# First attention of a 16-sample transformer kernel: weighed rows in two buffers in turn, and the product with the inverted sums two units later

## Chip, cores and metric

The kernel runs on one core of a Trainium2 chip. The metric is device time in microseconds of one execution of the whole program; before the change it was 1013.97 us, the median of three runs from 1012.39 to 1016.23 us.

## What is computed

A network of two layers on 16 samples of 256 tokens with 128 features, all in float32. Each layer modulates a layer norm, runs an attention, modulates again and runs a mixture of experts. The change lies in the attention of the first layer:

```python
xn = _ln(x, g_attn, b_attn)
qkv = (xn @ qkv_w + qkv_b)            # 16 heads of 8
scores = einsum("bhqd,bhkd->bhqk", q, k) / sqrt(HD)
scores = where(causal, -inf, scores)
attn_w = softmax(scores, axis=-1)
attn = einsum("bhqk,bhkd->bhqd", attn_w, v)
attn = attn @ out_w + out_b
```

What follows it in the layer (a residual, eight steps of a tanh recurrence, a feed-forward block and the experts) needs the attention of all samples in the order of the kernel's stages.

## The kernel before

Every engine has its own hand-written program; they meet at semaphores alone. Features lie on the 128 partitions, tokens in the columns. The samples are called batches, b = 0 to 15.

The first attention is one loop of 144 steps (`A_STEPS`), t = 0 to 143, that all engines walk through with the same counter. Eight steps make one batch; the step within a batch is the unit u = t % 8. A step handles two of the sixteen heads.

- TensorE. In step t it makes the row scores of two heads of batch t // 8 (`row_scores`, L445 and L452) into three PSUM banks in turn, and, 11 steps behind (`A_LAG`), the transposed scores of the same heads: first minus the maxima (`minus_maxima`, L465, the first instruction of a step in the rows below), then `key_scores` (L474, L477). `row_scores` waits for `a_mx`, the maxima three scores back, before it writes its bank. Behind these stands one more piece by unit: in even steps the weighing of values (`weigh`, L494), in u = 1 the transposition of the maxima (L418), in u = 3 the projection of values (L405), in u = 5 the projection of queries and keys of the next batch (`project_qk`, L388 and L389), in the steps of `OUT_STEPS` the output projection (`out_project`, L433), which waits for the product, `a_on`.
- VectorE. In step t it takes the maxima of the two heads (`maxima`, L1206 and L1208, each with a short read of the accumulator), 0.6 us a head. Ahead of the maxima of u = 4 stands `values` (L1229). Behind the maxima of the steps in `NORM_STEPS` stands `normalise` (L1244), called the product here: `ao = av * rec`.
- ScalarE. In step t it takes the exponentials of two transposed scores (`exps`, L918). Behind them stand, by step: `copy_maxima` (u = 1), `log_sums` (L932) and `exp_sums` (L936), which invert the sums as exp(-ln(x)), `keep_weighed` (L925, u = 4), which copies the weighed rows of batch b - 2 out of PSUM, `take_qk` (u = 5, L898 and L899), and `add_bias` (L940). TensorE's `minus_maxima` waits for an exponential of the step before.
- GpSimd. In step t it cuts the upper triangle from two heads' exponentials (`cut`, L1607, two instructions), and then masks queries of the next batch (`mask_queries`, L1616; u = 6 and 7, then 1 and 3) or adds a residual (L1621). The first step of a batch waits for the mask of u = 6 (`a_q`).
- SyncE's queue. The weighed rows hold values in 16 of every 32 partitions and their sums in the other 16. For batches 0 to 13 four DMAs (L297) move the sums beside the values, from `av` to `rec`, after `keep_weighed` (`a_cp`) and, as `rec` is one buffer, after the product of the batch before (`a_on`). For batches 14 and 15 VectorE does it with a shuffle (`spread_sums`, L1238). `log_sums` waits for the DMAs.

So the sums of a batch go: `keep_weighed` in u = 4, DMAs, logarithm in u = 0, exponential in u = 2, product in u = 3, output projection in u = 7 (batches 0 to 12, with the weighing two batches behind the row scores). `av`, `rec` and `ao` are one buffer each, 512 columns, in arrays that the layer norms use at other times.

Row scores end at step 127 (`A_UNITS`); steps 128 to 143 finish the transposed side. Batch 13 has its logarithm in step 128, exponential in 130, product and output projection in 131.

Of the kernel before, what the change touches and what calls it, by code (L numbers as in the profile page):

```python
# [14 lines left out]
ALU = mybir.AluOpType  # L15
ACT = mybir.ActivationFunctionType
# [3 lines left out]
BATCH, SEQ, D = 16, 256, 128  # L20
# [22 lines left out]
def adaln_kernel(nc, a):  # L43
    ctx = ExitStack()
    with ctx:
        def sb(name, shape, dt=FP32):
            return ctx.enter_context(nc.sbuf_tensor(name, shape, dt))

        def sem(name):
            return ctx.enter_context(nc.semaphore(name))  # L50
# [64 lines left out]
        sqb = sb("sqb", [P, 4, CH])  # L115
        rsb = sb("rsb", [P, 4, CH])
        xnb = sb("xnb", [P, 4, CH])
# [6 lines left out]
        mrow = sb("mrow", [P, 2, 3 * P], BF16)  # L124
        pr = sb("pr", [P, 6 * P])
        qs = sb("qs", [P, 2, SEQ])
        av, rec, ao = sqb[:, 0, :], rsb[:, 0, :], xnb[:, 0, :]

        lf, lw = qm[:, :, 0:2, :], qm[:, :, 2:4, :]
        av1, rec1, ao1 = sqb[:, 0:2, :], rsb[:, 0:2, :], xnb[:, 0, :]  # L130
# [28 lines left out]
        PS = ctx.enter_context(nc.psum_tensor("PS", [P, 8, CH], FP32))  # L159
# [14 lines left out]
        a_t, a_p, a_cut, a_av, a_cp, a_sh = [sem("a_" + n) for n in ("t", "p", "cut", "av", "cp", "sh")]  # L174
        a_moved = [sem(f"a_moved{n}") for n in range(2)]
        a_inv, a_on, a_pj, a_att, a_h = [sem("a_" + n) for n in ("inv", "on", "pj", "att", "h")]
# [30 lines left out]
        A_PST, A_PSO, A_PSM = 3, 6, 7  # L207
# [6 lines left out]

            return 4 + (q % 4 if q < 4 * STEPS else q % 2)

        NORM_STEPS = {8 * (b + 3) + 3 if b < BATCH - 2 else 8 * (b + 2) + 6: b for b in range(BATCH)}
        OUT_STEPS = {8 * (b + 3) + 7 if b < BATCH - 3 else 8 * (b + 3) + 3 if b < BATCH - 2 else 8 * (b + 2) + 7: b
                     for b in range(BATCH)}
        SPREAD_BY_DMA = BATCH - 2  # L220
        SPREAD_STEPS = {8 * (b + 2) + 5: b for b in range(SPREAD_BY_DMA, BATCH)}
        LOG_STEPS = {8 * (b + 3) if b < BATCH - 2 else 8 * (b + 2) + 5: b for b in range(BATCH)}
        EXP_STEPS = {8 * (b + 3) + 2 if b < BATCH - 2 else 8 * (b + 2) + 5: b for b in range(BATCH)}
        RESIDUAL_STEPS = {8 * (b + 4) + 2 if b < BATCH - 3 else 8 * (b + 3) + (5 if b < BATCH - 2 else 1): b
                          for b in range(BATCH - 1)}
        B_PSO, B_PSX = 6, 7
# [24 lines left out]
        def _(sp):  # L251
# [19 lines left out]
            for head in range(HEADS0):  # L271
                p = 32 * (head // 4) + HD0 * (head % 2)
# [11 lines left out]
            for head in range(HEADS1):  # L284
                p = 32 * (head % 4)
# [6 lines left out]
            for b in range(SPREAD_BY_DMA):  # L292
                sp.wait_ge(a_cp, b + 1)
                if b:
                    sp.wait_ge(a_on, b)
                for j in range(4):
                    sp.dma_start(rec[32 * j:32 * j + 16, :], av[32 * j + 16:32 * j + 32, :]).then_inc(a_moved[b % 2], 16)  # L297
            sp.wait_ge(a_av, 4 * BATCH)
            for dst, src in ((up0, a["up0"]), (gate0, a["gate0"])):
                sp.dma_start(dst, src).then_inc(ld_m0, 16)  # L300
# [556 lines left out]
        def _(act):  # L857
# [62 lines left out]

            def keep_weighed(b):
                act.wait_ge(a_av, 4 * b + 4)
                if b:
                    act.wait_ge(a_on, b)
                nc.scalar.activation(av[:, :], PS[:, A_PSO, :], ACT.Copy).then_inc(a_cp, 1)  # L925

            def log_sums(b):
                if b < SPREAD_BY_DMA:
                    act.wait_ge(a_moved[b % 2], 64 * (b // 2 + 1))
                else:  # L930
                    act.wait_ge(a_sh, b - SPREAD_BY_DMA + 1)
                nc.scalar.activation(rec[:, :], rec[:, :], ACT.Ln).then_inc(a_inv, 1)  # L932

            def exp_sums(b):
                act.wait_ge(a_inv, 2 * b + 1)
                nc.scalar.activation(rec[:, :], rec[:, :], ACT.Exp, scale=-1.0).then_inc(a_inv, 1)  # L936
# [6 lines left out]
            for t in range(A_STEPS):  # L943
                b, u, v = t // 8, t % 8, t - A_LAG
                if 0 <= v < A_UNITS:
                    exps(v)
                if u == 1 and 1 <= b <= BATCH:
                    copy_maxima(b - 1)
                if t in LOG_STEPS:
                    log_sums(LOG_STEPS[t])  # L950
                if t in EXP_STEPS:
                    exp_sums(EXP_STEPS[t])
                if u == 4 and b >= 2:
                    keep_weighed(b - 2)
                if u == 5 and b + 1 < BATCH:
                    take_qk(b + 1)
                if t in OUT_STEPS:
                    add_bias(OUT_STEPS[t])
# [155 lines left out]
        def _(dve):  # L1114
# [104 lines left out]
            def last_part(b):  # L1219
                dve.wait_ge(a_st, b + 1)  # L1220
                nc.vector.tensor_tensor(mxs[:, b % 2, :, :, :, 2], mxs[:, b % 2, :, :, :, 1], upper(b, 1),
                                        ALU.subtract).then_inc(a_sp, 1)
# [10 lines left out]
            def spread_sums(b):  # L1233

                dve.wait_ge(a_cp, b + 1)
                if b:
                    dve.wait_ge(a_on, b)
                nc.vector.stream_shuffle(rec[:, :], av[:, :], [16 + p % 16 for p in range(32)]).then_inc(a_sh, 1)  # L1238

            def normalise(b):  # L1240
                dve.wait_ge(a_inv, 2 * b + 2)
                if b:
                    dve.wait_ge(a_pj, b)
                nc.vector.tensor_tensor(ao[:, :], av[:, :], rec[:, :], ALU.mult).then_inc(a_on, 1)  # L1244

            dve.wait_ge(va_ones, 6)
            dve.wait_ge(mod_step, 10)
            for t in range(A_STEPS):
                b, u = t // 8, t % 8
                if t in SPREAD_STEPS:  # L1250
                    spread_sums(SPREAD_STEPS[t])
                if u == 4 and b < BATCH:
                    values(b)
                if t < A_UNITS:
                    maxima(t)
                if t == A_UNITS:
                    last_part(BATCH - 1)
                if t in NORM_STEPS:
                    normalise(NORM_STEPS[t])
                if u == 7 and b < BATCH:  # L1260
                    split_maxima(b)
# [509 lines left out]
```

## Time and profile before

| | |
|---|---|
| median of 3 runs | 1013.97 us |
| the profiled execution's own time | 1014.14 us |
| its span | 1012.3 us |
| instructions | 21410 |
| TensorE matmul busy | 930.3 us, 92% |
| VectorE busy | 616.3 us, 61% |
| ScalarE busy | 552.0 us, 55% |
| GpSimd busy | 460.2 us, 45% |
| granted TensorE clock, mean of the span | 0.989 |

Times in the rows are microseconds from the span's start, and every number is of one profiled execution. A busy TensorE is not TensorE at its peak: its matmuls are pipelined, and a short wait in the midst of a step may show as longer instructions instead of as idle time. The distance between the first L465 of two steps, a step's length, is the surer measure.

### The profile page before, as it was taken

Reading aid. Unit: us, or ns where it says so; the run is one execution under the profiler, and the core shown is the slowest. Engines: PE = TensorE matmul, PEld = TensorE weight load, DVE = VectorE, ACT = ScalarE, POOL = GpSimd, SP = SyncE. Lnnn points to the kernel's source line nnn. Section 1 sums busy time; section 2 is a strip of 40 time slices with the busy share of each in tenths; the row PEclk is TensorE's granted clock in tenths of the full one; section 3 lists DMA queues with packets and bytes.
Section 4 is the critical chain, followed back from the end, with each engine's and each line's share of the span. In section 5 each row is a group of like instructions: output and inputs, shape, how many; then the busy total and the mean of one; then the engine's idle time right before and its main releaser. Section 6 shows DMA issues by size and latency. Waiting matters only on the chain.

```text
span 1012.3 us, 21410 instructions
## 1 busy us (share of the span) xinstructions
PE 930.3 (92%) x7335; PEld 590.9 (58%) x7335; DVE 616.3 (61%) x2028; ACT 552.0 (55%) x1077; POOL 460.2 (45%) x697
## 2 busy tenths in 40 slices
PE   8999999999989979999887998889997899999997
PEld 4566677777654223334533886456664444399994
DVE  4788888888815966863633544577873653344444
ACT  6536666667657554565511554557785622255551
POOL 1146776776642946630074454335543044323331
PEclk9999999999999999999998999999999999999999
DMA  6720000000010000040011224100000000121115
GB/s 207 245 79 13 13 8 13 13 8 13 13 60 35 0 1 1 0 167 0 1 51 49 79 78 154 50 2 1 2 2 1 1 29 30 37 57 49 49 31 177
DMA packets 38617, 45.95 MB, mean 45 GB/s; under 512 B 7872, under 2 KB 31936, under 8 KB 37648
## 3 DMA queue, kind: packets, MB, share of 16 engines
q1 hardware_dynamic: 34000, 35.26, 11.4%
q0 software_dynamic: 4512, 9.32, 2.8%
q8 instruction: 62, 1.02, 0.4%
q14 instruction: 43, 0.35, 0.1%
HBM read 31.32 MB, written 18.69 MB: 49 GB/s over the span
## 4 chain that ended last, share of the span: by engine, by line
PE 78%; DVE 7%; ACT 6%; issue 4%; another core or an unknown queue 1%; DMA 1%; POOL 1%; DVEq 0%; SPq 0%; POOLq 0%
PE PS L697 6%; PE PS L452 5%; PE PS L494 5%; PE PS L680 5%; PE PS L687 5%; PE PS L348 4%; PE PS L465 4%; PE PS L640 3%; PE PS L357 3%; PE PS L631 3%; PE PS L633 3%; PE PS L554 2%; PE PS L445 2%; PE PS L790 2%; PE PS L809 2%
## 5 line engine op out<-in xcount | busy, mean ns | idle before, releaser
L918 ACT ACTIVATE pw<-PS 128x384 f32<-128x384 f32 x256 | 111.6, 488 | 73.0 <-PE PS L474 71.4
L1607 POOL TENSOR_SCALAR_AFFINE_SELECT pw<-pw 128x256 f32<-128x256 f32 x256 | 103.7, 429 | 75.8 <-ACT pw L918 74.6
L1206 DVE CUSTOM_DVE_ANT_0 PS<-PS,above 128x256 f32<-128x256 f32 x256 | 114.1, 446 | 38.4 <-PE PS L445 36.2
L1673 POOL DMA_INDIRECT token_rows<-xnb,slot_in x77 | 73.9, 959 | 114.2 <-ACT xnb L1032 107.6
L1659 POOL TENSOR_TENSOR XS<-XS,N 128x512 f32<-128x512 f32 x64 | 81.1, 1288 | 55.7 <-DVE N L1280 35.0
L452 PE MATMUL PS<-kf,qm 32*128 32x256 f32 x512 | 103.2, 426 | 0.5 <-POOL qm L1616 0.5
L1459 DVE TENSOR_TENSOR rsb<-sqb,PS 128x256 f32<-128x256 f32 (+1 forms) x77 | 42.6, 553 | 93.6 <-PE PS L687 44.8
L1208 DVE CUSTOM_DVE_ANT_0 PS<-PS,above 128x128 f32<-128x128 f32 x256 | 84.7, 331 | 0.0
L1629 POOL TENSOR_SCALAR_AFFINE_SELECT pw<-pw 128x256 f32<-128x256 f32 x128 | 56.0, 472 | 59.6 <-ACT pw L1077 59.6
L1015 ACT ACTIVATE sqb<-PS 128x512 f32<-128x512 f32 x48 | 28.7, 597 | 99.4 <-PE PS L631 80.6
L1370 DVE TENSOR_TENSOR rsb<-sqb,PS 128x512 f32<-128x512 f32 x48 | 32.9, 688 | 78.5 <-PE PS L633 55.9
L1616 POOL TENSOR_SCALAR qm<-qs,qmask 128x256 f32<-128x256 f32 x64 | 59.5, 931 | 43.8 <-ACT kf L899 43.8
L477 PE MATMUL PS<-qm,kf 32*128 32x256 f32 x512 | 76.3, 374 | 0.0
L1176 DVE TENSOR_TENSOR xnb<-PS,rsb 128x512 f32<-128x512 f32 x56 | 38.7, 691 | 56.5 <-ACT rsb L884 47.5
L1667 POOL DMA_INDIRECT sorted_rows<-H,pos x32 | 30.8, 964 | 79.7 <-DVE pos L1439 65.3
L1667 POOL DMA_INDIRECT sorted_rows<-region,pos x32 | 30.7, 959 | 77.1 <-DVE pos L1439 45.7
L680 PE MATMUL PS<-xnb,pw 128*128 128x128 f32 x460 | 64.1, 275 | 0.0
L687 PE MATMUL PS<-xnb,pw 128*128 128x128 f32 x460 | 63.9, 275 | 0.0
L970 ACT ACTIVATE PS<-PS,cols 128x512 f32<-128x512 f32 x64 | 42.2, 662 | 37.5 <-PE PS L554 22.3
L445 PE MATMUL PS<-kf,qm 32*128 32x128 f32 x512 | 61.7, 271 | 0.0
L445 PEld LDWEIGHTS PS<-kf,qm 32*128 32x128 f32 x512 | 60.7, 185 | 0.8
L554 PE MATMUL PS<-N,wxs 128*128 128x512 f32 x112 | 59.2, 615 | 2.0 <-DVE N L1289 0.4
(212 smaller groups left out, 2336.2 us busy)
## 6 DMA issues: line engine op xcount, KB each, us to landing
sorted_rows<-empty_rows_dram SPq DMA_DIRECT2D x2, 2535.0 KB, 14.7
slot_in<-sorted_rows SPq DMA_DIRECT2D x77, 65.0 KB
N<-token_rows SPq DMA_DIRECT2D x16, 256.0 KB, 5.0
X<-xT_dram SPq DMA_DIRECT2D x8, 256.0 KB, 5.2
token_rows<-empty_rows_dram SPq DMA_DIRECT2D x1, 2048.0 KB, 24.4
ATT<-gate_dram SPq DMA_DIRECT2D x1, 2048.0 KB
XS<-down_dram SPq DMA_DIRECT2D x1, 2048.0 KB
H<-up_dram SPq DMA_DIRECT2D x1, 2048.0 KB
```

The costliest lines, as they stand in the source:

```text
L445: nc.tensor.matmul(PS[:, bank, SEQ:SEQ + P], qm[r, b % 3, g, 0:P], kf[r, b % 3, 0:P], start=True, stop=True).then_inc(a_s, 1)
L452: nc.tensor.matmul(PS[:, bank, 0:SEQ], qm[r, b % 3, g, P:SEQ], kf[r, b % 3, :], start=True, stop=True)
L477: m = nc.tensor.matmul(PS[:, bank, 0:SEQ], kf[r, b % 3, 0:P], qm[r, b % 3, g, :], start=False, stop=True, skip_group_check=True)
L554: nc.tensor.matmul(PS[:, k, :], wxs[:, :], V[:, s], start=False, stop=True, skip_group_check=True).then_inc(i_p, 1)
L680: m = nc.tensor.matmul(PS[:, b, n * P:(n + 1) * P], wgate[:, b, n * P:(n + 1) * P], xnb[:, b, 0:P], start=True, stop=True)
L687: m = nc.tensor.matmul(PS[:, 2 + b, n * P:(n + 1) * P], wup[:, b, n * P:(n + 1) * P], xnb[:, b, 0:P], start=True, stop=True)
L918: nc.scalar.activation(pw[:, w % 2, j + n, :], PS[:, A_PST + (2 * v + n) % 3, 0:3 * P], ACT.Exp).then_inc(a_p, 1)
L1206: nc.vector.tensor_tensor_reduce(x[:, 0:SEQ], x[:, 0:SEQ], above[:, :], 1.0, -3e38, ALU.add, ALU.max, mxs[:, t // 8 % 2, 1, j, g, 0:1])
L1208: nc.vector.tensor_tensor_reduce(x[:, SEQ:SEQ + P], x[:, SEQ:SEQ + P], above[:, P:SEQ], 1.0, -3e38, ALU.add, ALU.max, mxs[:, t // 8 % 2, 0 ...
L1607: m = nc.gpsimd.affine_select(x[:, :, SEQ * k:SEQ * k + P], x[:, :, SEQ * k:SEQ * k + P], [[0, 2], [1, P]], ALU.is_ge, 0.0, base=0, channe ...
L1659: nc.gpsimd.tensor_tensor(XS[:, s], XS[:, s], V[:, s], ALU.add).then_inc(i_x, 1)
L1673: nc.gpsimd.indirect_dma_start(token_rows[l][:, :], bass.IndirectOffsetOnAxis(slot_in[:, r, D:D + 1].bitcast(mybir.dt.int32), 0), slot_out ...
```

## The change

`av` becomes two buffers in turn by batch. `keep_weighed` waits for the product of two batches before. The product goes from u = 3 to u = 5 for batches 0 to 12, and from step 131 to 130 for batch 13; the exponential of batch 13 goes from step 130 to 128. Batches 14 and 15 keep their steps (but batch 14 now lies in the other buffer).

```diff
-        av, rec, ao = sqb[:, 0, :], rsb[:, 0, :], xnb[:, 0, :]
+        av = [sqb[:, (b + 1) % 2, :] for b in range(BATCH)]
+        rec, ao = rsb[:, 0, :], xnb[:, 0, :]
...
-        NORM_STEPS = {8 * (b + 3) + 3 if b < BATCH - 2 else 8 * (b + 2) + 6: b for b in range(BATCH)}
+        NORM_STEPS = {8 * (b + 3) + (5 if b < BATCH - 3 else 2) if b < BATCH - 2 else 8 * (b + 2) + 6: b for b in range(BATCH)}
...
-        EXP_STEPS = {8 * (b + 3) + 2 if b < BATCH - 2 else 8 * (b + 2) + 5: b for b in range(BATCH)}
+        EXP_STEPS = {8 * (b + 3) + (2 if b < BATCH - 3 else 0) if b < BATCH - 2 else 8 * (b + 2) + 5: b for b in range(BATCH)}
...
-                    sp.dma_start(rec[32 * j:32 * j + 16, :], av[32 * j + 16:32 * j + 32, :]).then_inc(a_moved[b % 2], 16)
+                    sp.dma_start(rec[32 * j:32 * j + 16, :], av[b][32 * j + 16:32 * j + 32, :]).then_inc(a_moved[b % 2], 16)
...
             def keep_weighed(b):
                 act.wait_ge(a_av, 4 * b + 4)
-                if b:
-                    act.wait_ge(a_on, b)
-                nc.scalar.activation(av[:, :], PS[:, A_PSO, :], ACT.Copy).then_inc(a_cp, 1)
+                if b >= 2:
+                    act.wait_ge(a_on, b - 1)
+                nc.scalar.activation(av[b], PS[:, A_PSO, :], ACT.Copy).then_inc(a_cp, 1)
...
-                nc.vector.stream_shuffle(rec[:, :], av[:, :], [16 + p % 16 for p in range(32)]).then_inc(a_sh, 1)
+                nc.vector.stream_shuffle(rec[:, :], av[b], [16 + p % 16 for p in range(32)]).then_inc(a_sh, 1)
...
-                nc.vector.tensor_tensor(ao[:, :], av[:, :], rec[:, :], ALU.mult).then_inc(a_on, 1)
+                nc.vector.tensor_tensor(ao[:, :], av[b], rec[:, :], ALU.mult).then_inc(a_on, 1)
```

## Rows read from the trace of the kernel before

**Rows 1.** The page, part 4: the chain that ended last, shares by engine.
```profile
PE 78%; DVE 7%; ACT 6%; issue 4%; another core or an unknown queue 1%; DMA 1%; POOL 1%; DVEq 0%; SPq 0%; POOLq 0%
```
**Rows 2.** Timeline of TensorE, step 29: start, length, engine, line, operation, out<-in.
```profile
92.70 0.34 PE L465 MATMUL PS<-mrow,selb 32*128 32x384 bf16 x2
...
95.18 0.34 PE L465 MATMUL PS<-mrow,selb 32*128 32x384 bf16 x2
```
**Rows 3.** The same view, steps 21 and 22, before the first product.
```profile
78.38 0.34 PE L465 MATMUL PS<-mrow,selb 32*128 32x384 bf16 x2
...
80.36 0.33 PE L465 MATMUL PS<-mrow,selb 32*128 32x384 bf16 x2
```
**Rows 4.** Timeline of VectorE, end of step 27 and start of step 28.
```profile
91.48 0.76 DVE L1244 TENSOR_TENSOR xnb<-sqb,rsb 128x512 f32<-128x512 f32 x1
92.16 0.41 DVE L1229 TENSOR_TENSOR region<-PS,vb 128x256 f32<-128x256 f32 x1
92.50 0.42 DVE L1206 CUSTOM_DVE_ANT_0 PS<-PS,above 128x256 f32<-128x256 f32 x1
```
**Rows 5.** The same view, step 21 and the first maximum of step 22.
```profile
79.33 0.43 DVE L1206 CUSTOM_DVE_ANT_0 PS<-PS,above 128x256 f32<-128x256 f32 x1 [0.34 <-PE PS L445]
...
80.56 0.14 DVE L1208 DVE_READ_ACCUMULATOR2_ANT mxs<- 128x1 f32 x1
81.31 0.43 DVE L1206 CUSTOM_DVE_ANT_0 PS<-PS,above 128x256 f32<-128x256 f32 x1 [0.61 <-PE PS L445]
```
**Rows 6.** Timeline of GpSimd: cuts in step 21 and beside a product, a mask.
```profile
80.37 0.77 POOL L1607 TENSOR_SCALAR_AFFINE_SELECT pw<-pw 128x256 f32<-128x256 f32 x2 [0.93 <-ACT pw L918]
82.35 0.76 POOL L1607 TENSOR_SCALAR_AFFINE_SELECT pw<-pw 128x256 f32<-128x256 f32 x2 [1.22 <-ACT pw L918]
...
91.29 1.22 POOL L1607 TENSOR_SCALAR_AFFINE_SELECT pw<-pw 128x256 f32<-128x256 f32 x2 [0.94 <-ACT pw L918]
...
97.92 0.92 POOL L1616 TENSOR_SCALAR qm<-qs,qmask 128x256 f32<-128x256 f32 x1
```
**Rows 7.** Timeline of TensorE, first row of step 32.
```profile
98.90 0.33 PE L465 MATMUL PS<-mrow,selb 32*128 32x384 bf16 x2
```
**Rows 8.** Timeline of ScalarE: rows kept, logarithm, the exponentials behind it.
```profile
92.83 0.60 ACT L925 ACTIVATE sqb<-PS 128x512 f32<-128x512 f32 x1
...
100.72 0.63 ACT L932 ACTIVATE rsb<-rsb 128x512 f32<-128x512 f32 x1
101.78 0.87 ACT L918 ACTIVATE pw<-PS 128x384 f32<-128x384 f32 x2 [0.43 <-PE PS L474]
```
**Rows 9.** L297 on SyncE's queue: timeline, then issue and landing times of all 56.
```profile
93.45 3.06 SPq L297 DMA_DIRECT2D rsb<-sqb  x4
...
L297 SPq DMA_DIRECT2D rsb<-sqb x56: 507/589/983, 79.1 to 273.3; - x56
DMA to landing us min/median/max: 1.9/2.0/3.4
```
**Rows 10.** Timeline of TensorE: steps 33, 125 and 131.
```profile
100.61 0.34 PE L465 MATMUL PS<-mrow,selb 32*128 32x384 bf16 x2
...
102.41 0.34 PE L465 MATMUL PS<-mrow,selb 32*128 32x384 bf16 x2 [0.46 <-ACT pw L918]
...
270.69 0.34 PE L465 MATMUL PS<-mrow,selb 32*128 32x384 bf16 x2
...
272.92 0.34 PE L465 MATMUL PS<-mrow,selb 32*128 32x384 bf16 x2 [0.73 <-ACT pw L918]
...
283.24 1.13 PE L433 MATMUL PS<-xnb,wout 128*128 128x256 f32 x4 [0.65 <-DVE xnb L1244]
```
**Rows 11.** Timeline of ScalarE: exponentials of step 129, then the pair of step 133.
```profile
279.35 0.87 ACT L918 ACTIVATE pw<-PS 128x384 f32<-128x384 f32 x2 [0.32 <-PE PS L474]
...
287.80 0.63 ACT L932 ACTIVATE rsb<-rsb 128x512 f32<-128x512 f32 x1
...
289.00 0.85 ACT L918 ACTIVATE pw<-PS 128x384 f32<-128x384 f32 x2
```

## The prediction

> **What bounds the kernel now.** I read the page first: the chain that ended last is 78% matmul [rows 1], so a gain must shorten TensorE's own sequence. The change touches only the first attention, steps 0 to 143 (step 16 begins near 70 us, the stage ends near 304 us). There I read TensorE's timeline by the start of each step, which is the first L465 row of a step (t = 8b + u; u is the unit). A plain step is 1.7 us. In step 29 (u = 5) the start is at 92.70 and the next at 95.18, 2.48 us [rows 2]. Step 21 is the same unit with the same projection behind it, but comes before the first product, and takes 80.36 - 78.38 = 1.98 us [rows 3]. The 0.50 us between them is what the change can win in a batch.
>
> VectorE's timeline says where it comes from. The product of step 27 starts at 91.48, the value add of step 28 runs behind it, and the first maximum of step 28 starts at 92.50 [rows 4], so both take 1.02 us of VectorE. In a step with nothing else VectorE only has some 0.48 us to spare (0.34 us idle and a 0.14 us read that the next instruction may overlap) [rows 5]. The maxima of step 28 are therefore about 0.55 us late. They free the PSUM bank that the second row-score product of step 29 writes (TensorE waits for a_mx there), and everything after it in step 29 shifts: its transposed scores, then the projection, ScalarE's exponentials, the queries. TensorE is shown busy meanwhile; it is the step's length that gives the wait away.
>
> **The change, part by part.**
>
> Product of batches 0 to 11, from step u = 3 to u = 5 (steps 29, 37, ... 117): nothing is added, 0.77 us of VectorE moves. Taken away at u = 3 it leaves the value add (0.33 us) in a gap of 0.48 us: the maxima of u = 4 are on time and step u = 5 falls to 1.98 us. Put behind the maxima of u = 5 it finds the widest gap of the batch, because two projection passes sit between the scores of u = 5 and of u = 6: in step 21 the last read starts at 80.56 and the next maximum at 81.31 [rows 5], 0.75 us for an instruction whose successor starts 0.69 us later (91.48 to 92.16 by the value add, 0.77 us long itself). So it ends between 0.06 us before and 0.02 us after the next maximum is ready. Gain 0.50 us each, 12 x 0.50 = **6.0 us**. Bounds: 0.25 us if the new place costs half of what the old one did, 0.55 us if all the lateness comes back.
>
> GpSimd beside it. While the product of step 27 ran (91.48 to 92.25) the pair of cuts that began at 91.29 took 1.22 us; the pair at 80.37 in step 21 took 0.77 us [rows 6]. The product now starts at 80.56 of that clock against a pair at 80.37, the same 0.19 us behind, so the 0.45 us loss of GpSimd moves with it and does not grow. The next cuts wait for exponentials of u = 6 and start near 82.35, GpSimd being idle 1.22 us before them: that much cover for 0.45 us. Without that cover it would reach the mask of the next batch's queries, which does matter: the mask begun at 97.92 ends at 98.84, and step 32, whose scores need it, starts at 98.90 [rows 6, 7]. I cost it at nothing. The Trainium skill, SBUF - State Buffer, section "Who interferes with whom", says that a VectorE instruction with two SBUF inputs and a GpSimd instruction that reads SBUF exclude each other, and that the second to start blocks fully. By that the product would first wait 0.2 us for the running cut and end 0.1 to 0.2 us late for the maxima of u = 6; the row shows it only 0.08 us longer than the undisturbed one.
>
> Two buffers for the kept rows: the copy of batch b (L925, at 92.83 [rows 8]) waited for the product of b-1, which now comes two steps later; with the other buffer it waits for b-2, done a batch before. Cost nothing, same instruction. The cover is the buffer: with one, that copy, the first reader of the bank that the next weighing overwrites, would be stuck behind the product.
>
> The four DMAs that spread the sums (SP queue, one at a time) write the one buffer of inverted sums, so they still wait for the product of b-1. They started when the copy ended (93.45, step start + 0.75); they now start at the product's end, step start + 2.18 + 0.77 = + 2.95. From the first issue to the last landing: normally three issues of 0.59 and 2.0 us to land, 3.8 us; in this batch the issues took 3.06 us, so about 4.5 us [rows 9]. They land at + 6.8 to + 7.5. ScalarE wants them for the logarithm at 100.72, + 8.02 [rows 8], now + 7.52. It holds by 0.7 us, in the worst case seen by nothing, and behind the logarithm ScalarE sits idle 0.43 us. Cost 0; SP has nothing else queued there that is due before the stage ends.
>
> Product of batch 12, step 125: there is no projection in this step. Now it takes 272.92 - 270.69 = 2.23 us with TensorE waiting 0.73 us for ScalarE; a step of this kind with its wait for the exponentials and no late maxima is step 33, 1.80 us [rows 10]. Gain 0.43 to 0.55 us; I take **0.45**. Here the gap is a plain one of 0.48 us, so the product makes the maxima of step 126 late by 0.3 us. Their reader, the second score of step 127, has about that much to spare, since half of 0.55 us of lateness was absorbed at u = 5 too.
>
> Batch 13: exponential from step 130 to 128, product from 131 to 130, output projection unchanged at 131. TensorE waited 0.65 us there for the product [rows 10]; this goes. But logarithm and exponential now run back to back before the exponentials of step 129: such a pair takes 289.00 - 287.80 = 1.20 us, the logarithm alone 0.63 us, and the idle behind the lone logarithm in front of step 129 was 0.32 us [rows 11]. 1.20 - 0.63 - 0.32 = 0.25 us; TensorE waits for ScalarE in these steps, so this is given back. Net **0.40**. If the DMAs land late this is the place without slack.
>
> Sum: 6.0 + 0.45 + 0.40 = 6.85 us. What follows the stage (layer norms, recurrence, experts) hangs on its end in one chain and moves with it. The profiled execution took 1014.14 us for a span of 1012.3; that gives 1007.3. It lies 0.17 us over the median of the three runs, 1013.97. Forecast **1007.2 us**, 0.7% faster.
>
> **Rivals.**
>
> (a) The stall moves to u = 6 and 7: the product finishes late for the maxima of u = 6. For: the gap is 0.75 us for 0.69 to 0.77 us, and it shares with GpSimd. Against: 0.55 us of lateness costs 0.50 us today, so 0.1 us should hide wholly. If half comes back: 12 x 0.25 + 0.85 = 3.9 us, 1010.1. Chance 0.10.
>
> (b) GpSimd is held before the mask and step u = 0 starts 0.45 us later per batch: 12 x 0.05 + 0.85 = 1.5 us, 1012.5. It needs the product to run over the cuts of u = 6, over a microsecond later than I place it. Chance 0.04.
>
> (c) Slower: a ring product, DMA, logarithm, exponential, product through the single buffer of inverted sums. It decides when first issue to last landing takes more than 4.54 + 0.43 = 4.97 us, and makes the kernel slower beyond 5.5 us. If every batch had landings like the longest, 3.4 us, and issues as at 93.45 (2.5 + 3.4 = 5.9 us), it would lose 5.9 - 4.97 = 0.93 us a batch against a gain of 0.50: 12 x 0.43 = 5.2 us, less 0.8 at the tail, 4.4 us, 1018.4. Against: the median landing is 2.0 and the usual issue 0.59 us. Chance 0.03.
>
> (d) The lateness of step 28 has a second cause (the GpSimd collision of u = 3) or a hidden stall opens elsewhere by the shorter period, or the gain is larger, up to 9 us: 0.05.
>
> **How the numbers follow.** My case has 0.78. Its own spread is 12 x 0.05 from the product's place, 0.4 at the tail, and the runs, which lie 1.6 under and 2.3 us over their median: 1004.3 to 1009. The range takes in (a): 1004.0 to 1010.8, leaving out (b), (c) and part of (d). A measurement of this kernel can tell 0.5%, 5.1 us, so faster means under 1008.9: my case nearly whole, 0.82; within 0.5%: (a), (b) and a little of my case, 0.15; slower 0.03.
>
> **What would show it.** In the changed profile: a step u = 5 of 1.98 us; the product at step start + 2.2 and 0.77 us long, with a pair of cuts of 1.2 us beside it and the pair of u = 3 back at 0.77; the first maximum of u = 4 about 0.55 us earlier against its step; DMAs starting at + 3.0; a batch of 14.3 us where it is 14.8; no wait of the output projection at step 131. I would be wrong if ScalarE's idle before the logarithm names a DMA, if step u = 7 grows over 2.0 us, or if the maxima of u = 6 start late and step u = 6 or 7 takes the half microsecond back.

## The result and the profile after

The changed kernel takes 1007.71 us, the median of five runs from 1005.96 to 1009.27; the kernel before took 1013.9 (1012.39 to 1016.23, five runs). The ratio is 0.9931, 95% interval 0.9915 to 0.9946. On another chip, beside new runs of the kernel before, it was 0.9928 (0.9905 to 0.995). The profiled execution took 1005.96 us for a span of 1003.7. The kernel is 0.7% faster, as forecast. The ratios, here and below, leave out executions over 1.5% above the fastest of the same kernel, at a lower granted clock: one of eleven of the kernel before beside that second measurement, and two of ten of the kernel with the doubled product.

The change adds a line ahead of the functions, so L465 of before is L466 after, L1244 is L1245, and so on. TensorE's timeline, first row of steps 29, 30 and 32:

```profile
92.55 0.34 PE L466 MATMUL PS<-mrow,selb 32*128 32x384 bf16 x2
...
94.53 0.34 PE L466 MATMUL PS<-mrow,selb 32*128 32x384 bf16 x2
...
98.25 0.34 PE L466 MATMUL PS<-mrow,selb 32*128 32x384 bf16 x2
```

Step 29 is 1.98 us long, where it was 2.48 [rows 2], and equals step 21, which has no product [rows 3]. So are all twelve steps of this kind (29, 37, ... 117), each 1.98 against 2.48 or 2.49. VectorE's timeline around the value add of step 28 and the product, now in step 29:

```profile
91.33 0.42 DVE L1230 TENSOR_TENSOR region<-PS,vb 128x256 f32<-128x256 f32 x1
91.80 0.43 DVE L1207 CUSTOM_DVE_ANT_0 PS<-PS,above 128x256 f32<-128x256 f32 x1
...
94.73 0.76 DVE L1245 TENSOR_TENSOR xnb<-sqb,rsb 128x512 f32<-128x512 f32 x1
95.48 0.43 DVE L1207 CUSTOM_DVE_ANT_0 PS<-PS,above 128x256 f32<-128x256 f32 x1
```

The maxima of step 28 start at 91.80, 0.96 us after their step (90.84); before they started 1.52 us after it [rows 4]. The product runs from 94.73 to 95.49, and the next maximum starts at 95.48, 0.95 us after its step, on time to 0.01 us, with nothing left of the gap. GpSimd's timeline of the same moments:

```profile
91.14 0.76 POOL L1608 TENSOR_SCALAR_AFFINE_SELECT pw<-pw 128x256 f32<-128x256 f32 x2 [0.94 <-ACT pw L919]
...
94.54 1.22 POOL L1608 TENSOR_SCALAR_AFFINE_SELECT pw<-pw 128x256 f32<-128x256 f32 x2 [0.93 <-ACT pw L919]
96.52 0.77 POOL L1608 TENSOR_SCALAR_AFFINE_SELECT pw<-pw 128x256 f32<-128x256 f32 x2 [0.77 <-ACT pw L919]
97.27 0.92 POOL L1617 TENSOR_SCALAR qm<-qs,qmask 128x256 f32<-128x256 f32 x1
```

The collision has moved with the product: the pair of cuts beside it takes 1.22 us, the pair of u = 3 is back at 0.76 [rows 6]. GpSimd is idle 0.77 us behind it, so the mask that step 32 waits for is not touched: it ends at 98.19 and the step starts at 98.25.

ScalarE's logarithm of step 32, SyncE's queue (three of the four DMAs lie in the window asked for), and what the waits of the stage say of them (the last line is from the list of waits, 70 to 300 us: who waited for what, us in total, times, longest):

```profile
100.06 0.63 ACT L933 ACTIVATE rsb<-rsb 128x512 f32<-128x512 f32 x1
```
```profile
95.58 1.77 SPq L298 DMA_DIRECT2D rsb<-sqb  x3
```
```profile
ACT rsb L933 <- DMA rsb<-sqb: 0.2, 1, 0.2
```

The DMAs now start at 95.58, 3.03 us after step 29 began, and ScalarE asks for their data 7.51 us after it. It had to wait once in fourteen batches, for 0.2 us, and the step behind it (121) is 1.80 us long as before.

The end of the stage, TensorE's timeline, first rows of steps 126 to 132:

```profile
266.10 0.34 PE L466 MATMUL PS<-mrow,selb 32*128 32x384 bf16 x2 [0.71 <-ACT pw L919]
...
267.81 0.33 PE L466 MATMUL PS<-mrow,selb 32*128 32x384 bf16 x2
...
269.97 0.33 PE L466 MATMUL PS<-mrow,selb 32*128 32x384 bf16 x2
...
271.67 0.34 PE L466 MATMUL PS<-mrow,selb 32*128 32x384 bf16 x2
...
273.49 0.34 PE L466 MATMUL PS<-mrow,selb 32*128 32x384 bf16 x2 [0.55 <-ACT pw L919]
...
275.20 0.33 PE L466 MATMUL PS<-mrow,selb 32*128 32x384 bf16 x2
...
277.18 0.33 PE L466 MATMUL PS<-mrow,selb 32*128 32x384 bf16 x2
```

Step lengths, worked from the first L465 (L466) row of each step in both traces:

| step | before | after | gain |
|---|---|---|---|
| 29, 37, ... 117 (12 steps) | 2.48 to 2.49 | 1.98 | 6.1 |
| 125 | 2.23 | 1.69 | 0.54 |
| 127 | 1.98 | 2.16 | -0.18 |
| 129 | 1.58 | 1.82 | -0.24 |
| 131 | 2.69 | 1.98 | 0.71 |
| all others to 137 | | | within 0.02 each |

The sum is 6.9 us. The first layer norm behind the stage starts at 297.36 where it started at 304.49, 7.13 us earlier; 0.15 us of that is an earlier start of step 11. The spans differ by 8.6 us. The 1.5 us more lie behind the stage, where both kernels do the same. Two profiled executions of the changed kernel, on two chips, have the same stage to 0.02 us and spans of 1003.7 and 1000.1 us, so that part varies by more than 1.5 us without any change; the medians differ by 6.2. I take the stage's 6.9 us for the effect; what makes the rest was not tried.

### The profile page after: what moved, and what is told of

It reads as the page before. It is cut to its first block, busy times and chain, and to the rows that moved or that the text cites. A ratio compares the mean times of both kernels' runs of the same rounds, so it can differ in the third digit from the quotient of the medians.

```text
span 1003.7 us, 21409 instructions
## 1 busy us (share of the span) xinstructions
PE 924.3 (92%) x7335; PEld 588.0 (59%) x7335; DVE 615.5 (61%) x2028; ACT 552.2 (55%) x1077; POOL 460.4 (46%) x697
## 4 chain that ended last, share of the span: by engine, by line
PE 71%; issue 14%; ACT 6%; DVE 6%; POOL 1%; DMA 1%; DVEq 0%; SPq 0%; POOLq 0%; ACTq 0%
PE PS L698 6%; PE PS L453 5%; PE PS L495 5%; PE PS L681 5%; PE PS L688 5%; PE PS L466 4%; PE PS L349 4%; PE PS L358 3%; PE PS L641 3%; PE PS L632 3%; PE PS L634 3%; PE PS L555 2%; PE PS L810 2%; PE PS L791 2%; PE PS L446 2%
## 5 line engine op out<-in xcount | busy, mean ns | idle before, releaser
L453 PE MATMUL PS<-kf,qm 32*128 32x256 f32 x512 | 96.5, 426 | 0.5 <-POOL qm L1617 0.5
L1078 ACT ACTIVATE pw<-PS 128x768 f32<-128x768 f32 x64 | 48.4, 808 | 21.8 <-PE PS L794 21.8
L1033 ACT ACTIVATE xnb<-PS,slot_in 128x128 f32<-128x128 f32 x77 | 28.3, 367 | 57.5 <-PE PS L698 50.1
```

Source lines behind the costliest of these rows:

```text
L453: nc.tensor.matmul(PS[:, bank, 0:SEQ], qm[r, b % 3, g, P:SEQ], kf[r, b % 3, :], start=True, stop=True)
```

## The experiments

The experiments ran on two other chips of the kind, where the kernel before took some 1002 us. So times are told as ratios to the kernel before on the same chip, and steps are compared by their lengths, which agree to 0.02 us from chip to chip.

**The changed kernel once more.** No edit.

> The changed kernel itself, beside the experiments' chip, whose times for the kernel before are 1002 where the first chip had 1014. It leaves nothing out. If the gain is the stage's own (7.1 us shorter in the profiles) it is the same here: ratio 0.993 and steps u = 5 of 1.98 us. If the second chip's lower time comes from the same waits that the change removes, the gain is smaller, ratio over 0.997.

Measured: 0.9928 (0.9905 to 0.995), steps 29 to 30 at 92.56 and 94.54. The gain holds elsewhere. (This chip was none of the two of the other experiments; the kernel before took 1014.78 us there.)

**Two buffers alone.**

```diff
-        NORM_STEPS = {8 * (b + 3) + (5 if b < BATCH - 3 else 2) if b < BATCH - 2 else ...
+        NORM_STEPS = {8 * (b + 3) + 3 if b < BATCH - 2 else ...
-        EXP_STEPS = {8 * (b + 3) + (2 if b < BATCH - 3 else 0) if b < BATCH - 2 else ...
+        EXP_STEPS = {8 * (b + 3) + 2 if b < BATCH - 2 else ...
```

> Only the two buffers for the kept rows and the wait that goes with them; product and exponential where they were. My theory (the late maxima of u = 4 are the whole loss): steps u = 5 stay at 2.49 us from step 29 on, step 125 at 2.23, step 131 at 2.69, and the time stays that of the kernel before within 1 us, about 1014. Rival (the copy of the kept rows, no longer behind the product, is what frees ScalarE in u = 4 and 5): steps u = 5 at 1.98 us and about 1008.

Measured: ratio 0.9986 (0.9967 to 1.0005). Step 29 in TensorE's timeline:

```profile
92.69 0.34 PE L466 MATMUL PS<-mrow,selb 32*128 32x384 bf16 x2
...
95.18 0.34 PE L466 MATMUL PS<-mrow,selb 32*128 32x384 bf16 x2
```

2.49 us, as before, and the start of step 137 is at 293.21 where it was 293.22. The buffers bring nothing by themselves; the place of the product is the change.

**The product's place with one buffer.** `av` is one buffer, and the copy waits for the product of the batch before.

```diff
-        av = [sqb[:, (b + 1) % 2, :] for b in range(BATCH)]
+        av = [sqb[:, 0, :] for b in range(BATCH)]
-                if b >= 2:
-                    act.wait_ge(a_on, b - 1)
+                if b:
+                    act.wait_ge(a_on, b)
```

> The change with one buffer again, so that the copy of u = 4 waits for the product of u = 5. My theory: ScalarE, which should start the exponentials of u = 5 at step start + 1.05 us, first copies from + 3.0 to + 3.6 us (the product ends at + 2.95), so they are 2.5 us late and step u = 5 or 6 grows by about that in 13 batches: some 1040 us, slower than both kernels. Rival (the wait is covered, the second buffer buys nothing): 1008 us and steps u = 5 of 1.98.

Measured: ratio 1.0306 (1.0256 to 1.0356). ScalarE's timeline of step 28 and 29, then TensorE's of step 30:

```profile
91.93 0.87 ACT L919 ACTIVATE pw<-PS 128x384 f32<-128x384 f32 x2 [0.83 <-PE PS L475]
95.53 0.60 ACT L926 ACTIVATE sqb<-PS 128x512 f32<-128x512 f32 x1 [2.73 <-DVE xnb L1245]
96.03 0.87 ACT L919 ACTIVATE pw<-PS 128x384 f32<-128x384 f32 x2
```
```profile
96.66 0.34 PE L466 MATMUL PS<-mrow,selb 32*128 32x384 bf16 x2 [2.04 <-ACT pw L919]
```

The copy waits 2.73 us for the product; the exponentials queue behind it, and step 29 is 4.09 us long instead of 1.98, 2.11 us more (I had said 2.5). In thirteen batches that is 27 us; the profile's step 137 starts 36.6 us later than in the changed kernel. The rest, 9 us, is mostly in six of the steps u = 6, which take 2.9 to 3.2 us instead of 1.71 (step 38, for one, lies in a stretch, 110 to 116 us, with a granted clock of 0.78). So a stretch at a low clock follows five of twelve waits of TensorE of 2.04 us, and the last, of 3.10 us; behind the other seven step u = 6 takes its 1.71 us. The second buffer is what makes the new place possible, though it is worth nothing in the old one.

**The product one unit earlier, behind the maxima of u = 4.**

```diff
-        NORM_STEPS = {8 * (b + 3) + (5 if b < BATCH - 3 else 2) if ...
+        NORM_STEPS = {8 * (b + 3) + (4 if b < BATCH - 3 else 2) if ...
```

> The change with the product of batches 0 to 12 behind the maxima of u = 4 instead of u = 5. VectorE's gap there is 0.48 us for an instruction that takes 0.69, so the maxima of u = 5 come 0.21 us late. Theory from step 127 of the changed kernel (0.23 us late cost 0.18): 0.16 us in step u = 6 in 12 batches, 1.9 us more than the change, about 1009.6. The prediction's own figure (half of a lateness of 0.55 is absorbed, so 0.2 is hidden wholly): step u = 6 stays at 1.71 and 1007.7. Rival (what costs is the collision with GpSimd's cuts, wherever it falls outside of u = 5): 2.2 us in u = 6, about 1013.5.

Measured: ratio 0.9923 (0.9897 to 0.9949), like the change. VectorE's timeline, then TensorE's (steps 29, 30, 31):

```profile
93.09 0.78 DVE L1245 TENSOR_TENSOR xnb<-sqb,rsb 128x512 f32<-128x512 f32 x1
93.79 0.42 DVE L1207 CUSTOM_DVE_ANT_0 PS<-PS,above 128x256 f32<-128x256 f32 x1
```
```profile
92.61 0.33 PE L466 MATMUL PS<-mrow,selb 32*128 32x384 bf16 x2
...
94.59 0.33 PE L466 MATMUL PS<-mrow,selb 32*128 32x384 bf16 x2
...
96.30 0.34 PE L466 MATMUL PS<-mrow,selb 32*128 32x384 bf16 x2
```

The maxima of step 29 start 1.18 us after their step, 0.23 us late, and it costs nothing: step 30 is 1.71 us. My theory of that moment had carried over the price of step 127 (0.18 us for the same lateness), and fell. What it had missed is who reads: a late maximum of step t is read by the second row score of step t + 1. Behind the scores of u = 5 stands the projection of queries and keys, so step 30 begins 1.98 us after step 29 and not 1.71, and that adds 0.27 us of slack. Step 126, where no projection stands in step 125, is 1.89 us long in this kernel, 0.18 more than in the change. The prediction's own figure gave the right answer here for the wrong reason, as step 127 shows. The collision rival falls too: the cuts beside this product also take 1.22 us, at no cost.

**The value add out of the way, the product in its old place.** Built on the two buffers alone.

```diff
             for t in range(A_STEPS):
...
-                if u == 4 and b < BATCH:
-                    values(b)
                 if t < A_UNITS:
                     maxima(t)
+                if u == 4 and b < BATCH:
+                    values(b)
```

> Two buffers, product at u = 3 as in the kernel before, but the value add behind the maxima of u = 4 instead of in front of them. The product still runs over GpSimd's cuts of u = 3 (a pair of 1.22 us). Lateness theory: VectorE's queue in front of the maxima of u = 4 is 0.69 us in a gap of 0.48, they are 0.21 late and not 0.57, and step u = 5 loses 0.16 us, or up to 0.25 as the projection now waits for the value add: 2.15 to 2.25 us in place of 2.49, about 1010.5. Collision rival: step u = 5 stays at 2.49 and the time at 1014.

Measured: ratio 0.9969 (0.9943 to 0.9994). VectorE's timeline, GpSimd's, and TensorE's of steps 28, 29 and 30:

```profile
92.29 0.76 DVE L1245 TENSOR_TENSOR xnb<-sqb,rsb 128x512 f32<-128x512 f32 x1
92.97 0.42 DVE L1207 CUSTOM_DVE_ANT_0 PS<-PS,above 128x256 f32<-128x256 f32 x1
```
```profile
92.10 1.22 POOL L1608 TENSOR_SCALAR_AFFINE_SELECT pw<-pw 128x256 f32<-128x256 f32 x2 [0.93 <-ACT pw L919]
```
```profile
91.80 0.34 PE L466 MATMUL PS<-mrow,selb 32*128 32x384 bf16 x2
...
93.51 0.34 PE L466 MATMUL PS<-mrow,selb 32*128 32x384 bf16 x2
...
95.73 0.34 PE L466 MATMUL PS<-mrow,selb 32*128 32x384 bf16 x2
```

The collision of u = 3 is as it was, 1.22 us, and yet step 29 falls from 2.49 to 2.22 us. The maxima of step 28 are 0.22 us late (1.17 us after their step) instead of 0.57. So the length of VectorE's queue makes the loss; the collision by itself does not. (It has a small part in that length: beside the cuts VectorE gets to its next instruction 0.07 us later than alone, as the rows of the doubled product show.) Half of the change's gain is to be had without moving the product. Of the 0.24 us that are left, 0.04 belong to the value add, which the projection now waits for: step 21 of this kernel, with the value add moved and no product yet, takes 2.02 us where it takes 1.98 in all others.

**The product twice,** first into a part of `xnb` that nothing reads in this stage, then as in the change.

```diff
+                nc.vector.tensor_tensor(xnb[:, 1, :], av[b], rec[:, :], ALU.mult)
                 nc.vector.tensor_tensor(ao[:, :], av[b], rec[:, :], ALU.mult).then_inc(a_on, 1)
```

> The change with VectorE doing the product twice (first into a buffer that nothing reads there), at the same place. The computation is the same. The maxima of u = 6 come 0.69 us late. Lateness theory: all of it but 0.05 us in step u = 7, where the mask of the queries or the output projection may cover a part; the step grows from 2.02 by up to 0.64 us in 12 batches, at most 7.7 us: 1013 to 1015.5. Rival (u = 6 has slack of its own, which is why the product is free there): under 1010.

Measured: ratio 1.0065 (1.003 to 1.01). VectorE's timeline, then TensorE's (steps 30, 31, 32):

```profile
94.90 0.76 DVE L1245 TENSOR_TENSOR xnb<-sqb,rsb 128x512 f32<-128x512 f32 x1
95.58 0.89 DVE L1246 TENSOR_TENSOR xnb<-sqb,rsb 128x512 f32<-128x512 f32 x1
96.40 0.42 DVE L1207 CUSTOM_DVE_ANT_0 PS<-PS,above 128x256 f32<-128x256 f32 x1
```
```profile
94.70 0.34 PE L466 MATMUL PS<-mrow,selb 32*128 32x384 bf16 x2
...
96.40 0.33 PE L466 MATMUL PS<-mrow,selb 32*128 32x384 bf16 x2
...
99.09 0.33 PE L466 MATMUL PS<-mrow,selb 32*128 32x384 bf16 x2
```

The maxima of step 30 start 1.70 us after their step, 0.75 late, and step 31 is 2.69 us instead of 2.02. Neither the mask nor the output projection covers anything of it. The place at u = 5 has room for one product and no more. The time came out above the 1013 to 1015.5 us expected: the ratio times 1013.9 is 1020.5, its interval starts at 1017. In the profile, of the fastest of the ten executions, the stage is 9.8 us longer than in the change: 12 x 0.67, and what I had not counted, 0.81 in step 127, 0.21 in step 135 and 0.36 each in steps 57 (a group of DMAs landed late) and 113 (why is open).

The products of step 130, which have no cuts beside them, VectorE's timeline of the same kernel:

```profile
282.80 0.69 DVE L1245 TENSOR_TENSOR xnb<-sqb,rsb 128x512 f32<-128x512 f32 x1 [2.25 <-ACT rsb L937]
283.41 0.69 DVE L1246 TENSOR_TENSOR xnb<-sqb,rsb 128x512 f32<-128x512 f32 x1
```

Here the second product starts 0.61 us after the first. Beside the cuts it starts 0.68 us after it, and then takes 0.89 us instead of 0.69, since it begins while the long cut is still running (to 95.93). So part of these 0.75 us, 0.07 and 0.20, is the collision with GpSimd and not the second product's own length. What follows from the lateness does not hang on that.

Together with the others (lateness is the distance to 0.95 us behind the step's start):

| kernel, maxima of | late by | longer step | by |
|---|---|---|---|
| before, step 28 | 0.57 | 29 | 0.51 |
| value add later, step 28 | 0.22 | 29 | 0.24 |
| the change, step 126 | 0.23 | 127 | 0.18 |
| product at u = 4, step 29 | 0.23 | 30 | 0 |
| the change, step 30 | 0 | 31 | 0 |
| product twice, step 30 | 0.75 | 31 | 0.67 |

Where the reader follows in 1.7 us, lateness passes to TensorE all but 0.05 to 0.08 us of it (with the 0.04 us of the value add taken off, the second row has 0.20 for 0.22); behind a projection there is a quarter of a microsecond more.

**Batch 13 as before.** Exponential back in step 130, product in 131.

```diff
-        NORM_STEPS = {8 * (b + 3) + (5 if b < BATCH - 3 else 2) if ...
+        NORM_STEPS = {8 * (b + 3) + (5 if b < BATCH - 3 else 3) if ...
-        EXP_STEPS = {8 * (b + 3) + (2 if b < BATCH - 3 else 0) if ...
+        EXP_STEPS = {8 * (b + 3) + 2 if ...
```

> The change with batch 13's exponential and product back in steps 130 and 131. Theory: step 129 falls from 1.82 to 1.58 us, step 131 grows from 1.98 to 2.69, the stage is 0.47 us longer, everything else as in the change: 1008.2, which the times alone can't tell. Rival (the length of step 129 has to do with the DMAs of batch 13): step 129 stays at 1.8 us.

Measured: ratio 0.9927 (0.9903 to 0.9952). TensorE's timeline of steps 129 to 132:

```profile
271.78 0.33 PE L466 MATMUL PS<-mrow,selb 32*128 32x384 bf16 x2
273.36 0.34 PE L466 MATMUL PS<-mrow,selb 32*128 32x384 bf16 x2 [0.32 <-ACT pw L919]
275.07 0.33 PE L466 MATMUL PS<-mrow,selb 32*128 32x384 bf16 x2
...
277.76 0.34 PE L466 MATMUL PS<-mrow,selb 32*128 32x384 bf16 x2
```

Step 129 is 1.58 us, step 131 2.69: this part of the change brings 0.71 and costs 0.24 us, 0.47 net, in the steps alone; no time could tell it.

**The DMAs later.** SyncE's queue also waits for the maxima of u = 6, in a second kernel of u = 7 (`16 * b + 48`).

```diff
                 if b:
                     sp.wait_ge(a_on, b)
+                sp.wait_ge(a_mx, 16 * b + 46)
```

> The change, with SyncE's queue also waiting for the maxima of u = 6 before the four DMAs of a batch. They start 1.2 to 1.3 us later, at about + 4.25 us from the start of step u = 5; 3.8 us from first issue to last landing puts the sums at + 8.05 where ScalarE asks at + 7.52. That is 0.5 us late against 0.43 us of idle behind the logarithm. Theory: ScalarE's idle before the logarithm names a DMA, about 0.5 us in each batch, and a batch grows by 0.1 us or less: 1007.7 to 1009. Rival (the ring through the single buffer of inverted sums was near its bound already): a batch grows by more than 0.5 us, over 1014.

Measured: ratio 1.0162 (1.0115 to 1.0209). Times 1013.9 that is 1030 us, where 1007.7 to 1009 were expected; it lies on the rival's side, over 1014, though the usual batch does not grow by the rival's half microsecond. ScalarE's logarithms of three batches:

```profile
117.53 0.63 ACT L934 ACTIVATE rsb<-rsb 128x512 f32<-128x512 f32 x1 [0.57 <-DMA rsb<-sqb]
...
147.35 0.63 ACT L934 ACTIVATE rsb<-rsb 128x512 f32<-128x512 f32 x1 [1.47 <-DMA rsb<-sqb]
...
206.31 0.63 ACT L934 ACTIVATE rsb<-rsb 128x512 f32<-128x512 f32 x1 [1.66 <-DMA rsb<-sqb]
```

The usual batch is as I had worked it out: 0.57 us of wait (0.5 expected), step u = 1 at 1.95 us instead of 1.80, 0.15 more for the 0.1 expected. But four batches waited 1.4 to 1.7 us, and cost 1.0 to 1.2 us each in step u = 1 (a fifth waited 1.02 and cost 0.60), though the four issues took the usual 2.4 us: the last landing itself was 0.8 to 1.1 us later.

What these have in common stands in the list of DMA queues, asked for from the first issue to the last landing of the batch of 206.31 (201.4 to 206.4 us):

```profile
q8 instruction: 1, 0.02, 1.7%
```

A packet of 16 KB of the queue that the profile calls instruction moves in that time; the same question of the batch before 117.53, which landed on time, names no such queue. It holds throughout. Of the 616 DMAs of this kind in the eleven traces, 361 had no packet of the instruction queues (q8, q14) between issue and landing, and all of them landed within 2.01 us. The 157 that took longer, up to 3.62 us, all had one. Another 98 had one and landed within 2.01 us, so to have one is not enough. No run moves these packets, so this is a coincidence without an exception and not an experiment.

And the granted clock fell, which the table by stretches shows at the end of the stage:

```profile
272.00:279.00 7.00, 6.23 (x119) 4.80 (x112) 6.29 (x34) 4.06 (x10) 5.29 (x12) 1.00 0.02 4
279.00:286.00 7.00, 4.66 (x57) 3.24 (x52) 2.66 (x11) 4.31 (x10) 1.74 (x6) 1.00 0.10 21
286.00:300.00 14.00, 13.41 (x92) 8.52 (x92) 1.58 (x3) 6.73 (x15) 5.19 (x12) 0.51 0.00 1
300.00:317.00 17.00, 16.04 (x107) 9.50 (x100) 0.72 (x2) 5.30 (x12) 4.51 (x11) 0.50 0.06 10
```

(Columns: stretch, its length, busy time and number of TensorE's matmuls, weight loads, VectorE, ScalarE and GpSimd, clock, DMA share and GB/s.) Batch 13's sums were late as well (the logarithm waited 1.68 us, and the exponential stands right behind it, ahead of the exponentials that TensorE needs), so TensorE waited 2.34 us before step 130 and was busy for only 4.66 of the 7 us from 279 to 286. From 286 to 317 us it then has 0.50 to 0.51 of its clock, 1.2 GHz. Steps 130 to 136 take 21.88 us where the change takes 12.60. The start of step 137 is 20.5 us later than in the change (307.48 against 286.09, less 0.87 us by which step 24 starts later): 9.3 of these are the low clock of these steps, and the other 11.2 lie before step 130, mostly in the batches with late landings and the steps at a low clock behind two of them (the batches of 206.31 and 223.41). Behind the other two the clock stayed at 1.00; TensorE had waited 1.45 and 1.50 us there, and 1.69 and 1.67 in front of those two stretches.

> The change, with the DMAs of a batch waiting for the maxima of u = 7. They start at about + 6.0 us and land at + 9.8, 2.3 us later than ScalarE asks. Theory: with 0.43 us of idle behind the logarithm a batch grows by 1.8 us, in 13 batches 23 us, about 1031. Rival (TensorE's chain has other cover, such as the order of the exponentials): under 1015.

Measured, in one execution: 1054.19 us beside 1002.33 for the kernel before. Logarithms waited 37.3 us in fourteen batches, the batch's step u = 1 takes 3.62 to 4.64 us instead of 1.80; the fastest of them are the 1.8 us longer that I expected, the others, and the steps u = 2 behind most of them (2.3 to 3.2 us for 1.71), go with a granted clock of 0.90 in the mean from 80 to 200 us. By its ratio the change would take 995.4 us on this chip, so the cost is 59 us and not the 23 expected; the waits are 26 of it in fourteen batches (1.8 each), and I put the rest down to late landings and the clock, without having parted the two. It is one execution, but the size is far outside the spread of the others.

## Why the prediction was right

The main mechanism held. Step u = 5 was forecast at 1.98 us and is 1.98; the product at + 2.18 and 0.77 us long, and is at + 2.18 and 0.76; the cuts at 1.2, and are 1.22; the DMAs at + 3.0, and start at + 3.03; a batch at 14.3 us, and is 14.32 (106.87 - 92.55). Twelve steps brought 6.1 us of a forecast 6.0. The forecast of 1007.2 us met a median of 1007.71. (Its own sum, 1013.97 - 6.85, is 1007.12.) That the whole time met it to 0.5 us is in part luck: the stage brought 6.9 us, the medians differ by 6.2 and the profiled spans by 8.6. Two smaller terms were wrong, one in its reason (the steps 125 and 127) and one in its worst case (the DMAs).

- **Place of the product.** That the projection behind the scores of u = 5 makes the widest gap was right, though the product at u = 4 shows that the gap need not hold the product whole: its slack lies with the reader.
- **GpSimd.** Costed at nothing. GpSimd's own loss of 0.45 us cost nothing in three places (u = 3, 4 and 5); VectorE's loss of 0.07 us just fits into the gap at u = 5. The rule of the Trainium skill (SBUF - State Buffer, "Who interferes with whom") has the second to start fully blocked. The trace agrees only in part. The pair of cuts lasts 1.22 us, 0.45 longer, from 94.54 to 95.76; all of it is in the second cut, which starts after the product (0.86 us instead of 0.41) and ends 0.27 us after it, where a cut of 0.41 us held to the product's end (95.49) would end at 95.90. That the product itself would wait for the first cut to end is not seen: it took 0.76 us where the one without GpSimd beside it (step 130) took 0.69, and the next maximum was on time. That the collision cost nothing here hung on 0.01 us of the gap. A product that starts under a cut already made long loses more (the second of the doubled ones, 0.89 us for 0.69).
- **Second buffer.** Costed at nothing, with the stall that it avoids named and not priced. It is worth 2.11 us in a batch, and the stretches at a low clock besides.
- **Step 125 and 127.** Here a term was missized: "the product makes the maxima of step 126 late by 0.3 us. Their reader ... has about that much to spare, since half of 0.55 us of lateness was absorbed at u = 5 too." Nothing of the kind was absorbed: 0.57 us of lateness cost 0.51, as the prediction's own rival (a) says ("0.55 us of lateness costs 0.50 us today"). Step 127 is 0.18 us longer for 0.23. As I had taken 0.45 for a gain of 0.54, the net of 0.36 is near by luck, two errors that cancel, and rival (a) was cheap in the text for the same wrong reason: lateness of the maxima of u = 6 is paid nearly whole, as the doubled product shows.
- **Batch 13.** Forecast 0.65 - 0.25 = 0.40 us, measured 0.71 - 0.24 = 0.47.
- **The DMAs.** "In the worst case seen by nothing" was read from one batch, whose DMAs took 4.44 us from first issue to last landing. In the trace of before, four of the fourteen took 4.99 to 5.24 us, each with a packet of instructions beside it, and so more than rival (c)'s own point of decision, 4.97. There they had over 7 us of room and no wait showed them. At the new place, with 4.48 us of room (7.51 - 3.03) and 0.43 of idle, such a batch would lose up to 0.33 us, an estimate, too little to turn the result. In the changed kernel's trace only one batch was over the room (4.83 us). That the packets now fell elsewhere was not foreseen: luck, if a small piece.
- **Rival (c).** It didn't come about, and its point of decision for the usual batch (0.7 us of margin, 0.43 us of idle) was confirmed by the delayed DMAs. Its price was too low: I had not counted that stretches at the lower clock can follow TensorE's waits, which in the kernel with the DMAs behind u = 6 cost 9.3 us at the end of the stage alone.

What stays open: the 1.5 us of the profiled difference that lie behind the stage, whether the packets of instructions make the late landings or only go with them, and why the clock fell behind five of twelve waits of the same length in the kernel with one buffer.

## What to carry to other kernels

A short instruction of an engine that is far from busy can still cost the busiest engine most of its length (0.50 of 0.76 us here), if it stands in front of work that frees a buffer; look for the step where the reader of that buffer comes latest, and put it there. Read such a loss as the distance between like steps with and without the instruction, since no idle row shows it. When an instruction is moved past a copy in another engine, the buffer between them has to be doubled first, and the doubling shows no gain until then (0.9986 alone). When a DMA's landing is given a margin, take the slowest of all its landings in the trace, and not the one beside the row that is read.

## What the runs showed of the hardware

A pair of cuts on GpSimd that meets a two-input product on VectorE takes 1.22 us instead of 0.76 or 0.77, at each of the three places tried, all of it in the cut that starts after the product (0.86 us instead of 0.41). The product beside it takes 0.76 to 0.78 us instead of 0.69 and holds up the next instruction by 0.07 us; one that started while the long cut was running took 0.89.

Of the DMAs of 32 KB from SBUF to SBUF the median lands in 2.0 us. None of the 361 without a packet of the instruction queues beside it took over 2.01 us; all 157 that took longer, up to 3.62 us, had one (eleven traces). Such a packet of 16 KB moves for 0.88 to 1.52 us.

A wait of TensorE of 2.34 us, after steps that were nearly full, left it busy for 4.66 of 7 us and was followed by 31 us at 1.2 GHz (0.50 to 0.51 of the clock), in which the same steps took 21.88 us instead of 12.60; the changed kernel keeps 2.4 GHz there, at 6.45 of 7 us busy (271 to 278 us). The wait cost nine more that way. It is not so after each wait: in the same kernel waits of 1.67 and 1.69 us were followed by some 4 us at the low clock and waits of 1.45 and 1.50 us by none, and with one buffer five of twelve waits of 2.04 us were.
